# A three-stage transformer kernel: seven masked products in the first mixture, betas by accumulating transfers, one key-value product on VectorE and LayerNorm statistics on ScalarE

## The chip, the cores and the metric

The kernel runs on one core of one Trainium2 chip. A core has five engines that run their own instruction lists and wait for each other by semaphores: TensorE (PE) for matrix products, VectorE (DVE), ScalarE (ACT), GpSimd (POOL) and SyncE (SP), which here only issues transfers. The metric is the device time of one execution in microseconds; the median of 3 runs of the kernel before is 938.53 us (938.17 to 942.1).

## The reference, cut to what matters

The input is 16 sequences of 512 tokens with 128 features. Four blocks follow each other, each with an adaptive LayerNorm ahead of it:

```python
x = L0_attn_x                       # (16, 512, 128)
# block 1: a linear recurrence over the tokens, gated, then LayerNorm with gamma and beta
h = _layernorm(x) * (1 + ca) + sa
x = x + ga * _L0_attn_ref(h, A, Bp, Cp, Dp, Wg, bg, gamma, beta)
# block 2: a mixture of 8 experts, one of them for each token
h = _layernorm(x) * (1 + cb) + sb
sel = argmax(softmax(h @ gate_w + gate_b))
x = x + gb * (h @ expert_w[sel] + expert_b[sel])
# block 3: causal linear attention, 16 heads of 8
h = _layernorm(x) * (1 + ca) + sa
q, k, v = softplus(h @ Wq.T + bq), softplus(h @ Wk.T + bk), h @ Wv.T + bv
kv, k1 = cumsum(k[..., :, None] * v[..., None, :]), cumsum(k)
x = x + ga * ((einsum(q, kv) / sum(q * k1)) @ Wo.T + bo)
# block 4: a mixture of 8 experts with two per token, swiglu, 256 hidden
h = _layernorm(x) * (1 + cb) + sb
```

The scale and shift vectors (`sa`, `ca`, `ga`, `sb`, `cb`, `gb`) are one row of 128 per sequence. `_layernorm` takes mean and variance over the 128 features of a token.

## The kernel before

A sequence is C = 4 tiles of 128 tokens. `x_tok` holds all of x, 128 tokens by 64 tiles by 128 features, in SBUF for the whole kernel. There are five phases, each a block of engine lists with a barrier behind it, and within a phase the lists are written out by hand in the order in which each engine works.

**Phase 1 (0 to about 101 us)** builds the powers of the state matrix and the gated, normalised input. `roots(i)` on GpSimd (L241, L243) takes the square roots of the variances for a group of four sequences, four times. **Phase 2 (to 147 us)** is the recurrence as Toeplitz products, in 16 groups of U = 4 features' matrices. For each group VectorE spreads the ends of chunks over `carry` in three copies (L666), and TensorE multiplies them (L706).

**The first mixture (147 to 345 us)** joins block 1's output to x and does block 2 for one sequence w after the other. VectorE: `statistics` of block 1's output (L1007, L1011), `gamma` (L1035 in the head, L1040 later: normalised times ga*gamma), `joined` (L1050 in the head, L1054 later: add to x_tok), `stats_x` (L1018, L1022), `shift_x_head` (L1027), `best` (L1061 to L1073: add the gate's bias to the logits, find the largest, make a one-hot `hot`), and `mask(w, e)` (L1091): the sequence's features `f_t` times the one-hot row of expert e, which has been spread over all partitions in `wide`. `added` (L1082) adds the experts' output. TensorE: `turn` (L1125, transposes of the normalised tokens), `logits` (L1133), `turn_hot` (L1141), `bias` (L1157, the one-hot times the experts' biases, split into three bf16 pieces), `product(w, e)` (L1161, expert e's weights times masked features, accumulated over e in PSUM) and `turn_back` (L1149). Each product shows as two instructions in the profile. GpSimd has four-column means and scales for the later LayerNorms (L844 to L867) and `beta(w)` (L884), which adds the row ga*beta to x_tok. ScalarE: `squares` with accumulated sums (L925), `norm_y`, `norm_x` (L949, L959), `feat` (L967) and `scaled` (L980). In the head, before the first product, TensorE does idle products (L70) between its steps. SyncE loads the rows ga*gamma and ga*beta of each sequence four ahead (`rows`), all weights at the phase's start, and sends each one-hot to DRAM and back (`kept`, `spread`).

**Attention (345 to 707 us)** is a loop over n = 0 to 20 in which each step works on several sequences at once: the step names below carry the lag. VectorE, in the list's order: `weighted(n-1, 0)` (L1983, queries times running key-value sums in PSUM), `denominators` (L1989), `correction(n)` (L1994, a part of softplus), `weighted(n-1, 1)`, `logits(n-5)` (L2076) with the choice of two experts, `corrected`, `softplus(n)` (L2001, L2007), `residual(n-2)` (L2032: x_tok gets the attention's output), `weighted(n-1, 2)`, `states(n)`, `shifted(n-3)` (L2051), `gated` (L2065), `weighted(n-1, 3)`, `moments(n-2)` (L2038, L2044: mean and variance of the four tiles), then `first_cum` (L2013), `added`, `modulated(n-3)` (L2057, L2059) and `divided(n-1)` (L1974). GpSimd makes four key-value products per sequence, `products(w, c)` (L1641), c = 0 to 3, and sends the tokens' rows by indirect transfers, `send` (L1650). TensorE turns each product into running sums, `sums(w, c)` (L2450), 16 half products. ScalarE, among others: `payload` (L1715, L1717), `turned_pay` (L1834), `norm0` (L1723), `normed` (L1821), `variance_log` and `variance_root` (L1692, L1697: the LayerNorm scale from `moments`) and `squares` of the next norm (L1803).

**The second mixture (707 to 943 us)** runs 71 tiles of tokens sorted by expert.

## Time and profile before

| | us |
|---|---|
| median of 3 runs | 938.53 (938.17 to 942.1) |
| the profiled execution's own time | 945.22 |
| its span, on which all rows stand | 943.4 |

| stretch, us from the span's start | what | length | PE busy | DVE busy | ACT busy | POOL busy |
|---|---|---|---|---|---|---|
| 0 to 147.3 | phases 1 and 2 | 147.3 | 124.7 | 106.0 | 63.0 | 17.9 |
| 147.3 to 178.6 | first mixture, head | 31.3 | 26.8 | 30.0 | 14.0 | 14.9 |
| 178.6 to 337.6 | first mixture, products | 159.0 | 152.5 | 146.5 | 113.2 | 100.6 |
| 337.6 to 345.0 | its end | 7.4 | 5.5 | 0.9 | 2.3 | 1.7 |
| 345.0 to 440.4 | attention, first turns | 95.4 | 90.7 | 75.3 | 62.4 | 40.8 |
| 440.4 to 643.8 | attention, ten full turns | 203.4 | 192.7 | 190.7 | 147.2 | 166.4 |
| 643.8 to 707.0 | attention, last turns | 63.2 | 51.6 | 57.3 | 34.7 | 50.2 |
| 707.0 to 943.4 | second mixture | 236.4 | 213.9 | 167.4 | 181.3 | 174.1 |

An engine's busy time is the time in which it executed. TensorE's matmuls overlap, so the start of the next tells its pace better than a duration does. Where TensorE does idle products, its busy time says nothing about need.

### The profile page before, as it was taken

To read this page: it belongs to the slowest core of one execution; us is meant where nothing else is said; L and a number is where in the kernel's file an instruction comes from. 1 tells how busy PE (TensorE), PEld (TensorE's weight loads), DVE (VectorE), ACT (ScalarE), POOL (GpSimd) and SP (SyncE) were. 2 spreads that over 40 slices of the span, in tenths; PEclk is the share of its full clock that TensorE was granted. 3 is DMA by queue.
4 is the path that set the end of the run, shared out by engine and by line. 5 is a ranking of instruction groups with operands and counts; after the bars stand their busy time and mean duration, and the time that the engine had idled before them with its cause. 6 is when DMAs were issued, how large, how long until landed. Compare 5 with 4: busy or idle time off the path is not lost.

```text
span 943.4 us, 24125 instructions
## 1 busy us (share of the span) xinstructions
PE 858.5 (91%) x7676; PEld 674.7 (72%) x7692; DVE 774.1 (82%) x2369; ACT 618.2 (66%) x1603; POOL 566.4 (60%) x547
## 2 busy tenths in 40 slices
PE   6979898998999989999999999999879999999990
PEld 5945576645445458888778877787668888888890
DVE  3988787999999736988999999999886866666996
ACT  3557123487888446467677777666557888888880
POOL 1211004277776414443888888888777777777773
PEclk9989999899999999999999999999998999999996
DMA  5330262233223203001111112111227766756987
GB/s 155 95 95 1 67 204 59 104 110 141 102 101 130 99 3 96 15 17 35 43 52 49 49 54 64 53 50 49 66 68 219 219 183 183 228 181 196 338 263 248
DMA packets 93962, 105.82 MB, mean 112 GB/s; under 512 B 16095, under 2 KB 75802, under 8 KB 91661
## 3 DMA queue, kind: packets, MB, share of 16 engines
q1 hardware_dynamic: 81884, 84.59, 29.3%
q0 software_dynamic: 8640, 17.97, 5.3%
q10 hardware_dynamic: 3312, 1.70, 0.6%
q8 instruction: 64, 1.05, 0.5%
q14 instruction: 62, 0.50, 0.2%
HBM read 79.91 MB, written 24.32 MB: 110 GB/s over the span
## 4 chain that ended last, share of the span: by engine, by line
PE 48%; DVE 8%; issue 2%; ACT 2%; DMA 2%; POOL 1%; SPq 0%; ACTq 0%; DVEq 0%; POOLq 0%
PE ps L2694 12%; PE ps L2450 10%; PE ps L2717 6%; PE ps L2466 2%; PE ps L2513 2%; PE ps L2441 2%; PE ps L2416 2%; PE ps L2677 2%; PE ps L2567 2%; PE ps L2551 2%; PE ps L2429 1%; DVE qk L2001 1%; DVE qk L2007 1%; PE ps L2461 1%; DMA parts<-gx,dest 1%
## 5 line engine op out<-in xcount | busy, mean ns | idle before, releaser
L1641 POOL TENSOR_TENSOR kvb<-qk,v 128x1024 f32<-128x1024 f32 x64 | 127.3, 1995 | 68.8 <-DVE qk L2007 48.9
L1650 POOL DMA_INDIRECT rows_of<-payb,posu x128 | 144.3, 1128 | 40.1 <-issue 27.5
L2450 PE MATMUL ps<-con,kvb 128*128 128x128 f32 x1024 | 126.0, 276 | 0.0
L1161 PE MATMUL ps<-masked,ew 128*128 128x512 f32 x256 | 123.3, 610 | 1.9 <-DVE masked L1091 1.8
L2450 PEld LDWEIGHTS ps<-con,kvb 128*128 128x128 f32 x1024 | 119.4, 192 | 1.0 <-issue 1.0
L2378 DVE TENSOR_SCALAR qk<-ps,b 128x256 f32<-128x256 f32 x142 | 62.1, 478 | 49.7 <-PE ps L2694 44.6
L1674 POOL DMA_INDIRECT parts<-h,dest x72 | 80.6, 1119 | 23.3 <-issue 20.1
L1674 POOL DMA_INDIRECT parts<-gx,dest x70 | 78.7, 1125 | 21.3 <-issue 19.2
L1091 DVE TENSOR_TENSOR masked<-f_t,wide 128x512 f32<-128x512 f32 x128 | 85.9, 715 | 4.9 <-PE ps L1161 4.7
L1983 DVE TENSOR_TENSOR qc<-ps,qk 128x1024 f32<-128x1024 f32 x64 | 78.0, 1218 | 9.3 <-PE ps L2450 8.2
L1161 PEld LDWEIGHTS ps<-masked,ew 128*128 128x128 f32 x256 | 44.8, 192 | 44.9 <-issue 30.0
L2717 PE MATMUL ps<-w,f_t 128*128 x568 | 75.1, 275 | 0.0
L2717 PEld LDWEIGHTS ps<-w,f_t 128*128 128x128 f32 x568 | 69.0, 192 | 8.2
L1888 ACT ACTIVATE qk<-ps,b 128x256 f32<-128x256 f32 x142 | 59.6, 470 | 18.3 <-PE ps L2694 17.9
L2694 PE MATMUL ps<-qd,ex 128*128 128x256 f32 x288 | 69.8, 386 | 0.0
L2694 PE MATMUL ps<-qd,lg 128*128 128x256 f32 x280 | 66.2, 379 | 0.0
L70 PE MATMUL ps<-con 128*128 128x128 f32 x398 | 56.3, 293 | 5.5 <-PEq L75 3.9
L70 PEld LDWEIGHTS ps<-con 128*128 128x128 f32 x398 | 51.4, 204 | 9.6 <-issue 6.8
L2694 PEld LDWEIGHTS ps<-qd,ex 128*128 128x128 f32 x288 | 53.0, 194 | 6.0
L1893 ACT ACTIVATE nrm<-qk,limit 128x512 f32<-128x512 f32 x71 | 51.3, 722 | 6.8
L2267 DVE SCALAR_TENSOR_TENSOR f_t<-qk,nrm 128x512 f32<-128x512 f32 x71 | 49.2, 693 | 6.8 <-DVE qk L2378 0.5
L2694 PEld LDWEIGHTS ps<-qd,lg 128*128 128x128 f32 x280 | 50.5, 190 | 5.4
(370 smaller groups left out, 2107.0 us busy)
## 6 DMA issues: line engine op xcount, KB each, us to landing
wide<-hot_dram SPq DMA_DIRECT2D x16, 1024.0 KB, 4.6
kvb<-rows_of SPq DMA_DIRECT2D x71, 132.0 KB, 2.5
ex<-in_w_dram SPq DMA_DIRECT2D x36, 256.0 KB
lg<-in_w_dram SPq DMA_DIRECT2D x35, 256.0 KB
toep<-taps_dram SPq DMA_DIRECT2D x16, 512.0 KB, 4.5
xg<-parts SPq DMA_DIRECT2D x16, 512.0 KB, 5.2
x_tok<-in_x_dram SPq DMA_DIRECT2D x16, 256.0 KB, 2.9
rb<-den_dram SPq DMA_DIRECT2D x64, 64.0 KB
```

Of the source, the lines that this page charges most:

```text
L70: nc.tensor.matmul(ps[:, bank, 0:P], k("ident"), k("ident"), start=True, stop=True)
L1091: nc.vector.tensor_tensor(masked[e % 4][:, :], f_t[w % W][:, :], wide[w % W][:, e, :], ALU.mult).then_inc(s["masked"], 1)
L1161: nc.tensor.matmul(ps[:, w % 2, :], ew0[:, e, :], masked[e % 4][:, :], start=False, stop=(e == E - 1)).then_inc(s["product"], 1)
L1641: nc.gpsimd.tensor_tensor(kv[g % KB][:, :, :].rearrange("p e (h d) -> p e h d", h=H), k_in, v_in, ALU.mult).then_inc(s["kv"], 1)
L1650: nc.gpsimd.indirect_dma_start(rows_of, bass.IndirectOffsetOnAxis(ap=posu[w % PR][:, slot, t:t + 1], axis=0), pay[w % PB][:, t, :], None). ...
L1674: nc.gpsimd.indirect_dma_start(parts, bass.IndirectOffsetOnAxis(ap=dest[:, at, c:c + 1], axis=0), yw[u][:, c, :], None).then_inc(s_out[u], 16)
L1888: last = nc.scalar.activation(glu[v % 2][:, f, :], ps[:, bank, f * SP:(f + 1) * SP], ACT.Relu, bias=b1[:, bass.ds(e * NF + f, 1)], scale=-1.0)
L1983: nc.vector.tensor_tensor(qc[g % 2][:, :, :], cum(g), q_in, ALU.mult).then_inc(s["qc"], 1)
L2378: last = nc.vector.tensor_scalar(lin[v % 2][:, f, :], ps[:, bank + 1, f * SP:(f + 1) * SP], b1[:, bass.ds(e * NF + 2 + f, 1)], 8.0, ALU.ad ...
L2450: last = nc.tensor.matmul(cum(g)[:, e, :], kv[g % KB][:, e, :], k("upto"), start=True, stop=True)
L2694: last = nc.tensor.matmul(ps[:, bank + f // 2, (f % 2) * SP:(f % 2 + 1) * SP], w1c[v % WC][:, f * P:(f + 1) * P], x_t[v % 2][:, :], start= ...
L2717: last = nc.tensor.matmul(to, act_t[v % 2][:, j, c * P:(c + 1) * P], w2[:, bass.ds(e * (2 * D) + j * D, D)], start=False, stop=(c == S - 1 ...
```

## The change

In phase 1 and at ten places GpSimd now issues `add_beta(b)`, a transfer that adds the row ga*beta to the four tiles of sequence b in x_tok as it writes (b = 0 to 9): five ahead of the last `roots` and five behind. The other six are `late_beta` transfers in the first mixture; `joined(w)` for w from 10 waits for all six. `beta` on GpSimd is gone, and the row load brings only ga*gamma.

In phase 2 the three carry copies are one. The mixture's weights and biases are loaded and prepared here, and GpSimd subtracts the last expert's weights from the seven others' (128 x 896). The mixture then computes the last expert's product for all tokens, unmasked (`base`), and seven masked products with the differences. The gate's bias enters by a bf16 product ahead of the logits, so `best` reads PSUM. The lists of all five engines are in a new order.

In attention `last_product(n-1)` on VectorE makes the fourth key-value product. `moments` is gone; ScalarE makes sums, negative means and centred squares of the tokens instead.

```diff
+                    def add_beta(b):
+                        pool.wait_ge(s_nt, b + 1)
+                        nc.gpsimd.dma_start(x_tok[:, b * C:(b + 1) * C, :], bass.AP(rows_tensor, (b * len(ROWS) + 1) * D, [[0, P], [0, C], [1, D]]),
+                                            accum_op=ALU.add).then_inc(betas_added, 16)
+                    for i in range(NI - 1):
                         roots(i)
+                    pool.wait_ge(s_rout, 16)
+                    for b in range(U + 1):
+                        add_beta(b)
+                    roots(NI - 1)
+                    for b in range(U + 1, EARLY_BETAS):
+                        add_beta(b)
...
-                                for c in range(1, C):
-                                    src = by_chunk(ends[u][:, :], c - 1)
-                                    last = nc.vector.tensor_tensor(
+                                src = ends[u][:, :].rearrange("p (b c) -> p b c", c=C)[:, :, 0:C - 1]
+                                nc.vector.tensor_tensor(
...
+                    pool.wait_ge(s_ahead, 6 * 16)
+                    nc.gpsimd.tensor_tensor(ew0[:, 0:M, :], ew0[:, 0:M, :], ew0[:, M:E, :].to_broadcast([P, M, D]), ALU.subtract).then_inc(s_ew, 1)
...
-                    def beta(w):
-                        if exists(w):
-                            landed(pool, s_rows, w)
-                            nc.gpsimd.tensor_tensor(tiles(x_tok, w), tiles(x_tok, w), rows[w % W][:, 1:2, :].to_broadcast([P, C, D]), ALU.add).then_inc(s["beta"], 1)
+                    def late_beta(w):
+                        nc.gpsimd.dma_start(tiles(x_tok, w), bass.AP(rows_tensor, (w * len(ROWS) + 1) * D, [[0, P], [0, C], [1, D]]),
+                                            accum_op=ALU.add).then_inc(s["late_betas"], 16)
...
+                            if w >= EARLY_BETAS:
+                                dve.wait_ge(s["late_betas"], (B - EARLY_BETAS) * 16)
                             done(dve, "gamma", w)
-                            done(dve, "beta", w)
...
-                            nc.vector.tensor_tensor(logit[:, :, :], ps[:, LOGIT, 0:C * E].rearrange("p (t e) -> p t e", e=E),
-                                                    gb0[:, :, :].to_broadcast([P, C, E]), ALU.add).then_inc(s["lg"], 1)
...
+                    def base(w):
+                        done(pe, "moe_t", w - 2)
+                        done(pe, "feat", w)
+                        nc.tensor.matmul(ps[:, w % 2, :], ew0[:, M, :], f_t[w % W][:, :], start=True, stop=False).then_inc(s["plain"], 1)
...
+                    def row_sums(w):
...
+                            for c in range(C):
+                                last = nc.scalar.activation(unread[:, c, :], tile(w, c), ACT.Copy, accum_out=sx[:, c:c + 1])
+                    def centred_squares(w):
...
+                            for c in range(C):
+                                last = nc.scalar.activation(unread[:, c, :], tile(w, c), ACT.Square, bias=nm[w % 2][:, c:c + 1], accum_out=vs[w % 2][:, c:c + 1])
...
                         payload(n - 7)
+                        row_sums(n - 5)
+                        negative_means(n - 5)
+                        centred_squares(n - 5)
                         turned_pay(n - 7)
...
+                    def last_product(w):
...
+                            nc.vector.tensor_tensor(kv[g % KB][:, :, :].rearrange("p e (h d) -> p e h d", h=H), k_in, v_in, ALU.mult).then_inc(s["kv_last"], 1)
...
                         denominators(n - 1)
+                        last_product(n - 1)
                         correction(n)
...
                         weighted(n - 1, 3)
-                        moments(n - 2)
```

The order at three places. First VectorE at the start of the first mixture, before:

```order
L1007 BN_STATS halves<-xg 128x6 x4
L1011 BN_AGGR moments<-halves 128x2 x4
L1007 BN_STATS halves<-xg 128x6 x4
L1011 BN_AGGR moments<-halves 128x2 x4
L1035 SCALAR_TENSOR_TENSOR yn_88<-xg,moments,rows_73 128x128 x4
L1050 SCALAR_TENSOR_TENSOR x_tok<-yn_88,stat_77,x_tok 128x128 x4
L1018 BN_STATS halves_x<-x_tok 128x6 x4
L1022 BN_AGGR moments_x<-halves_x 128x2 x4
L1035 SCALAR_TENSOR_TENSOR yn_89<-xg,moments,rows_74 128x128 x4
L1027 SCALAR_TENSOR_TENSOR stat_82<-moments_x,stat_81 128x4
L1050 SCALAR_TENSOR_TENSOR x_tok<-yn_89,stat_77,x_tok 128x128 x4
```

The same place now (`statistics`, `gamma`, `joined`, `stats_x` are L1036 and L1040, L1064, L1080, L1047 and L1051):

```order
L1036 BN_STATS halves<-xg 128x6 x4
L1040 BN_AGGR moments<-halves 128x2 x4
L1064 SCALAR_TENSOR_TENSOR yn_93<-xg,moments,rows_79 128x128 x4
L1080 SCALAR_TENSOR_TENSOR x_tok<-yn_93,stat_83,x_tok 128x128 x4
L1047 BN_STATS halves_x<-x_tok 128x6 x4
L1051 BN_AGGR moments_x<-halves_x 128x2 x4
L1036 BN_STATS halves<-xg 128x6 x4
L1040 BN_AGGR moments<-halves 128x2 x4
L1056 SCALAR_TENSOR_TENSOR stat_88<-moments_x,stat_87 128x4
L1064 SCALAR_TENSOR_TENSOR yn_94<-xg,moments,rows_80 128x128 x4
L1080 SCALAR_TENSOR_TENSOR x_tok<-yn_94,stat_83,x_tok 128x128 x4
```

The second sequence's statistics moved from ahead of the first gamma to behind the first sequence's stats_x.

Second, TensorE where one sequence's products end and the next one's begin, before:

```order
L1161 MATMUL ps<-masked_106,ew_65 128x512
L1161 MATMUL ps<-masked_107,ew_65 128x512
L1125 MATMUL ps<-con,xn_90 128x128 x4
L1161 MATMUL ps<-masked_108,ew_65 128x512
L1161 MATMUL ps<-masked_109,ew_65 128x512
L1133 MATMUL ps<-gw_71,f_t_92 128x8 x4
L1157 MATMUL ps<-hot_b_98,ebx 128x512
L1149 MATMUL ps<-con,moe_t_105 128x128 x4
L1161 MATMUL ps<-masked_106,ew_65 128x512
L1161 MATMUL ps<-masked_107,ew_65 128x512
```

The same now (L1191 the masked products, L1183 `base`, L1158 the gate's bias, L1187 the experts' bias):

```order
L1191 MATMUL ps<-masked_114,ew_5 128x512
L1152 MATMUL ps<-con,xn_95 128x128 x4
L1191 MATMUL ps<-masked_111,ew_5 128x512
L1191 MATMUL ps<-masked_112,ew_5 128x512
L1183 MATMUL ps<-f_t_99,ew_5 128x512
L1158 MATMUL ps<-gb_13,one_14 128x32
L1161 MATMUL ps<-gw_18,f_t_97 128x8 x4
L1187 MATMUL ps<-hot_b_103,ebx 128x512
L1177 MATMUL ps<-con,moe_t_110 128x128 x4
L1191 MATMUL ps<-masked_113,ew_5 128x512
```

The next sequence's accumulation, which began with the bias product L1157, now begins with the unmasked product L1183.

Third, attention. VectorE from the fourth weighting of one sequence to the second of the next, before (L1989 the denominators, L1994 the correction):

```order
L2038 BN_STATS st<-x_tok 128x6 x4
L2044 BN_AGGR mv_174<-st 128x2 x4
L2013 TENSOR_TENSOR qd<-ps,qk_189 128x512
L2070 TENSOR_TENSOR x_tok<-x_tok,gx_210 128x512
L2027 TENSOR_TENSOR skv_199<-skv_199 128x144 x2
L2057 TENSOR_TENSOR h_208<-h_208,rows_168 128x512
L2059 TENSOR_TENSOR h_208<-h_208,rows_168 128x512
L1974 TENSOR_TENSOR g_t<-ps,rb_202 128x512
L1983 TENSOR_TENSOR qc_195<-ps,qk_189 128x1024
L1989 RECIPROCAL rden_201<-ps 96x128
L1994 SCALAR_TENSOR_TENSOR ex<-lg,ex 128x1024
L1983 TENSOR_TENSOR qc_196<-ps,qk_189 128x1024
```

The same now (L2045 is `last_product`, L2051 the denominators, L2056 the correction):

```order
L2075 TENSOR_TENSOR qd<-ps,qk_191 128x512
L2119 TENSOR_TENSOR x_tok<-x_tok,gx_214 128x512
L2089 TENSOR_TENSOR skv_201<-skv_201 128x144 x2
L2106 TENSOR_TENSOR h_212<-h_212,rows_171 128x512
L2108 TENSOR_TENSOR h_212<-h_212,rows_171 128x512
L2025 TENSOR_TENSOR g_t<-ps,rb_206 128x512
L2034 TENSOR_TENSOR qc_198<-ps,qk_191 128x1024
L2051 RECIPROCAL rden_203<-ps 96x128
L2045 TENSOR_TENSOR kvb<-qk_191,v_195 128x1024
L2056 SCALAR_TENSOR_TENSOR ex<-lg,ex 128x1024
L2034 TENSOR_TENSOR qc_199<-ps,qk_191 128x1024
```

The statistics and aggregates went, and one 128 x 1024 product stands between the denominators and the correction.

ScalarE in the same turn, from the payload on, before:

```order
L1715 ACTIVATE payb<-h_209,rm_183 128x128 x4
L1717 ACTIVATE payb<-place 128x4
L1834 ACTIVATE p_t<-ps 128x512
L1723 ACTIVATE nrm_184<-x_tok,shift_61,rs_60 128x128 x4
L1730 ACTIVATE ex<-ps,bq 128x512
L1821 ACTIVATE h_208<-x_tok,sh_180,rv_177 128x128 x4
```

And now (L1714, L1722 and L1729 are the sums, negative means and centred squares, L1882 the turned payload):

```order
L1761 ACTIVATE payb<-h_212,rm_186 128x128 x4
L1763 ACTIVATE payb<-place 128x4
L1714 ACTIVATE unread,sx<-x_tok 128x128 x4
L1722 ACTIVATE nm_174<-sx 128x4
L1729 ACTIVATE unread,vs_176<-x_tok,nm_174 128x128 x4
L1882 ACTIVATE p_t<-ps 128x512
L1769 ACTIVATE nrm_187<-x_tok,shift_75,rs_74 128x128 x4
L1776 ACTIVATE ex<-ps,bq 128x512
L1869 ACTIVATE h_211<-x_tok,sh_183,rv_180 128x128 x4
```

The three new rows stand between the payload and its turn.

## Rows read from the trace of the kernel before

**Rows 1.** Busy time by stretch: length, then busy us and instructions of each engine.

```profile
147.30:178.60 31.30, 26.83 (x176) 23.78 (x176) 29.95 (x122) 14.03 (x36) 14.86 (x21) 0.84 0.32 101
178.60:337.60 159.00, 152.54 (x543) 75.75 (x543) 146.53 (x527) 113.20 (x357) 100.64 (x164) 0.99 0.28 106
```

**Rows 2.** In time: start, us, engine; and a line's group: busy us, mean ns.

```profile
75.86 0.26 POOL L241 TENSOR_SCALAR rstd<-mv 128x16 f32<-128x16 f32 x1 [20.03 <-DVE mv L261]
...
L1650 POOL DMA_INDIRECT rows_of<-payb,posu x128 | 144.3, 1128 | 40.1 <-issue 27.5
```

**Rows 3.** In time, the mixture's head: VectorE and GpSimd.

```profile
150.31 2.55 POOL L884 TENSOR_TENSOR x_tok<-x_tok,rows 128x512 f32<-128x512 f32 x2 [2.60 <-DMA rows<-rows_dram]
150.97 2.74 DVE L1035 SCALAR_TENSOR_TENSOR yn<-xg,moments,rows 128x128 f32<-128x128 f32 x4
...
159.42 4.93 POOL L884 TENSOR_TENSOR x_tok<-x_tok,rows 128x512 f32<-128x512 f32 x4
...
162.00 2.37 DVE L1027 SCALAR_TENSOR_TENSOR stat<-moments_x,stat 128x4 f32<-128x4 f32 x1
164.29 1.44 DVE L1035 SCALAR_TENSOR_TENSOR yn<-xg,moments,rows 128x128 f32<-128x128 f32 x4
...
177.88 4.30 DVE L1091 TENSOR_TENSOR masked<-f_t,wide 128x512 f32<-128x512 f32 x7
```

**Rows 4.** In time, TensorE in the mixture.

```profile
248.93 0.60 PE L1125 MATMUL ps<-con,xn 128*128 128x128 f32 x4
249.36 1.88 PE L1161 MATMUL ps<-masked,ew 128*128 128x512 f32 x4
251.08 0.99 PE L1133 MATMUL ps<-gw,f_t 128*128 128x8 f32 x8
252.00 0.38 PE L1157 MATMUL ps<-hot_b,ebx 24*128 24x512 bf16 x1
```

**Rows 5.** In time, VectorE in the mixture.

```profile
243.55 0.18 DVE L1061 TENSOR_TENSOR logit<-ps,gb 128x32 f32<-128x32 f32 x1
...
257.82 4.76 DVE L1091 TENSOR_TENSOR masked<-f_t,wide 128x512 f32<-128x512 f32 x6
```

**Rows 6.** In time, one turn of attention.

```profile
524.99 0.19 DVE L2076 TENSOR_TENSOR logit<-ps,gb 128x32 f32<-128x32 f32 x1 [0.30 <-PE ps L2616]
...
530.00 0.68 DVE L2032 TENSOR_TENSOR x_tok<-x_tok,ps 128x512 f32<-128x512 f32 x1
530.23 0.97 PE L2567 MATMUL ps<-v,qk 128*128 128x144 f32 x6 [0.90 <-DVE qk L2007]
533.59 0.60 ACT L1834 ACTIVATE p_t<-ps 128x512 f32<-128x512 f32 x1 [3.99 <-PE ps L2538]
534.86 0.86 DVE L2038 BATCH_NORM_STATS2 st<-x_tok 128x6 f32<-128x128 f32 x4
538.15 1.95 PE L2450 MATMUL ps<-con,kvb 128*128 128x128 f32 x16
539.72 1.98 POOL L1641 TENSOR_TENSOR kvb<-qk,v 128x1024 f32<-128x1024 f32 x1
540.13 1.22 DVE L1983 TENSOR_TENSOR qc<-ps,qk 128x1024 f32<-128x1024 f32 x1
543.80 1.22 DVE L1983 TENSOR_TENSOR qc<-ps,qk 128x1024 f32<-128x1024 f32 x1 [0.50 <-PE ps L2450]
545.32 0.19 DVE L2076 TENSOR_TENSOR logit<-ps,gb 128x32 f32<-128x32 f32 x1 [0.30 <-PE ps L2616]
```

**Rows 7.** ScalarE's accumulating passes, grouped by line: busy us, mean ns, idle before.

```profile
L925 ACT ACTIVATE junk<-x_tok,stat 128x128 f32<-128x128 f32 x112 | 43.3, 388 | 13.4 <-DVE x_tok L1082 11.5 <-DVE x_tok L1054 1.8
L925 ACT ACTIVATION_READ_ACCUMULATOR junk<-x_tok,stat 128x1 f32 x112 | 21.0, 187 | 0.0
L1803 ACT ACTIVATE junk<-h 128x128 f32<-128x128 f32 x64 | 18.8, 298 | 3.7 <-DVE h L2059 3.7
```

**Rows 8.** In time, ScalarE in attention's last turns.

```profile
682.80 0.60 ACT L1834 ACTIVATE p_t<-ps 128x512 f32<-128x512 f32 x1 [0.86 <-PE ps L2538]
```

384 lines of the change are left out of this document (201 added, 183 removed).

## The prediction

> **What bounds the kernel now.** I read four views in this order. The busy times by stretch say which engine fills a stage. The instructions in order of time say who waits for whom there. The groups by line give the price of one instruction. The groups' idle columns bound what a wait is worth.
>
> The first mixture has two parts. In its head, from the barrier at 147.3 to the first product at 178.6, VectorE is busy 29.95 of 31.30 us and nothing else fills the time [rows 1]: the head ends when VectorE has worked through its list. From 178.6 to 337.6 TensorE (152.54) and VectorE (146.53 of 159.00) are both nearly full [rows 1]. To see which one sets the pace, take starts and not modelled busy times: four half products go by in 251.08 - 249.36 = 1.72 us, 0.43 each; four transposes take 0.43, the logits 0.92, and the bias product at most its 0.38 [rows 4]. I take 0.31 for that one, where the next start falls. A sequence is 16 halves (6.88), three sets of transposes (1.3), logits and bias: 9.4 us. Less what is done in the head, that is about 144 us of TensorE work in 159; the 15 us over are waits on VectorE. VectorE's list is about 149 us, of which 5.6 are stalls: six masks from 257.82 took 4.76 where seven from 177.88 took 4.30, so 0.61 each and 3.67 for six [rows 3, 5]; 1.09 us went while GpSimd added a beta. Five such places and a small one make 5.6.
>
> In attention the same turn repeats from 524.99 to 545.32, 20.33 us [rows 6]; eleven such turns are in the steady part. The ring: the state product on TensorE waits 0.90 us for a VectorE product at 530.23; from there TensorE runs on to the sums that end at 540.10, the first weighting on VectorE starts at 540.13, the second at 543.80 after 0.50 us of waiting, the logits at 545.32 after 0.30 [rows 6]; from there VectorE's list runs without a gap to the product that releases the next state product. Whatever sits on VectorE between 540.1 and 545.3 beyond those small waits lengthens every turn.
>
> **Phase 1: nothing.** Five accumulating transfers go on GpSimd ahead of its last square root, which starts at 75.86 after 20.03 us of idling [rows 2]. Their cost there is not in the trace. The nearest row is the indirect transfer, 128 descriptors in 1.128 us [rows 2]; these have 512 short rows each, so at most 4 x 1.128 = 4.5 us, 5 x 4.5 = 22.6. The fifth sequence is ready about 15 us before 75.86 and the shift that reads the root comes near 80: the queue is done in time, or within 3 us of it. Below: 0, above: +3. I take 0, since 4 x is already a price for four whole transfers.
>
> **Phase 2: nothing.** Three carry copies become one, which shortens VectorE's part of each group; but TensorE sets the pace of the scan, and VectorE waits for it in every group. That same slack covers what the weight differences, the bias pieces and the six loads on GpSimd and SyncE might hold up. If the cover went, a held VectorE would show as carry waits on TensorE; I keep +-0.5 us for it.
>
> **Mixture, head: -3.1.** Three rows show what beta on GpSimd costs VectorE. The first gamma took 2.74 us, a later one of the same shape 1.44 (1.3 lost); a shift of four columns took 2.37 us while GpSimd ran four betas from 159.42 (2.2 lost) [rows 3]; smaller ones make 3.9. Also gone are two logit additions (0.4), one shift that goes behind the first masks (0.25), and the wait for a constant at the start (0.4): -5.0. Against it, one statistics is no longer ahead of the first gamma, so gamma waits for its row, which lands at 150.3 [rows 3], about 1.0; and the shorter list meets the roots of ScalarE sooner, about 0.9. The first product moves from 178.6 to 175.5.
>
> The Trainium skill ("SBUF — State Buffer", the section on the port pair that VectorE and GpSimd share) says that a GpSimd operation and a VectorE operation with two SBUF inputs exclude each other for a whole instruction; rows 3 agree (2.37 us for a tiny one). By that rule the gain of taking betas off GpSimd is real, and it speaks against the product that attention puts on VectorE.
>
> **Mixture, products: -11.5.** VectorE loses 16 masks (16 x 0.61 = 9.8), 14 further logit additions at 0.2 (2.9) [rows 3, 5] and the 5.6 of stalls: 149 becomes about 131. TensorE keeps all halves: the unmasked product with the last expert's weights is one of the eight. Two of the plain products move into the head (2 x 0.86 = -1.7), the gate bias adds 14 small products, about +1. TensorE needs about 143.5, VectorE 131: TensorE becomes the bound, and only waits for single masks or hot rows stay, for which I leave 4 us. 159.0 becomes 147.5. Six late transfers sit in GpSimd's queue among means and scales; each up to 4.5 us [rows 2]. If they cost that, roots and with them normalised rows come late for two or three sequences. Bounds of the term: -14 (2 us of waits) and -4 (most waits replaced). I choose near the upper third, because the plain products give TensorE work exactly when masks are not there yet.
> Mixture: -3.1 - 11.5 = -14.6.
>
> **Attention: +6.6.** The fourth key-value product moves from GpSimd, where one takes 1.98 us [rows 6], to VectorE. There it is of the weighting's shape (128 x 1024, at most 1.22 us); I take 1.15. It stands behind the denominators and ahead of the correction, so in the stretch above: 1.15 - 0.50 delays the second weighting by 0.65, and the logits by 0.35 after their 0.30. The moments, 0.86 for the statistics at 534.86 and a third of one for the aggregates, leave VectorE, but just ahead of 540.13, where it waits for TensorE's 540.10 anyway [rows 6]: they buy nothing there. Part of the 0.35 is taken up behind, since the VectorE list from 545 to 530 is no longer held by GpSimd's fourth product. I count 0.25.
>
> ScalarE gets sums, means and centred squares. Four accumulating passes without bias at 0.298 and four with bias at 0.388, their read-outs overlapped [rows 7], and a small one of 0.2: by durations 4 x 0.298 + 0.2 + 4 x 0.388 = 2.9, with the two hand-overs about 3.2 us. They can start when the residual is written, 530.00 + 0.68 = 530.7, and stand ahead of the payload's turn, which before ran at 533.59 after 3.99 us of idling [rows 6]: 2.9 us of room. The 0.3 over goes on to the normalised tokens and is nearly eaten before 540.1: 0.05. Together 0.3 a turn, 11 turns: +3.3. The first turns, in which engines are less full, +0.6. In the last turns there is no filling work: at 682.80 the turned payload starts after only 0.86 us of idling [rows 8], so the block's 3.2 us delays it by some 2.7 once, and routing's last logits behind it. +3.3 + 0.6 + 2.7 = +6.6, between +3 (tail +0.5, turns +0.2) and +10 (0.6 a turn).
>
> GpSimd's third product ends at 541.70 and the new one on VectorE can't start before weighting and reciprocal, near 542.2 [rows 6]. A turn in which GpSimd is 0.5 us later makes VectorE wait.
>
> **Sum.** 0 + 0 - 14.6 + 6.6 = -8.0. The profiled run's own time is 945.2 (span 943.4 and 1.8 around it); it becomes 937.2. The median of the runs shown is 938.5, 6.7 under it; the same difference gives 930.5. The second mixture is untouched.
>
> **Rivals.** (a) The mixture gives only the head and little more: the late transfers cost near 4.5 us each and TensorE waits at other places instead. -3.1 - 4.5 = -7.6, total 938.5 - 7.6 + 6.6 = 937.5. For it: GpSimd's chain for a sequence is already four steps long. Against it: VectorE gets 18 us of room. 0.22.
> (b) The new product costs attention nothing but the tail (0.1 a turn, +3.3 in all), and the mixture fills TensorE (-17): 938.5 - 17 + 3.3 = 924.8. 0.20.
> (c) Slower: the statistics on ScalarE are longer than their room. If each of the eight read-outs adds to its pass instead of lying beneath it, the block is 4 x 0.487 + 0.2 + 4 x 0.575 = 4.5 us by bounds from [rows 7], 1.6 over the room; the normalised tokens, their modulation and the division follow, and the first weighting starts 1.3 later each turn: 11 x (1.3 + 0.25) + 3.3 = +20, total 938.5 - 14.6 + 20 = 943.9; with (a)'s mixture 951. It decides from a block of about 4.0 us. Against it: 64 passes without and 112 with a bias now run back to back with no idle time ahead of a read-out [rows 7]. 0.09.
> (d) The transfers don't do what they say on time: an accumulating transfer takes over 4.7 us on GpSimd, and the last root and its shift come late, +3 to +8: 933.5 to 938.5. 0.05.
>
> **How the numbers follow.** The forecast, 930.5 with its own range of 926.5 to 934, has 0.44. 0.5% of the median, about what a measurement of this kernel can tell from no change, is 4.7: the bounds are 933.8 and 943.2. Forecast and (b) are faster, and a small part of (a) and (d): 0.44 + 0.20 + 0.03 = 0.67. The rest of (a) and (d), and (c) at its mildest, within half a percent: 0.24 + 0.01 = 0.25. Slower: what is left of (c), 0.08. The range reaches from (b) to behind (a): 923 to 941.
>
> **What would show it.** Right: the first product near 175.5 and products over 147 to 149 us; the VectorE operations of the head back at 1.44 and 0.13; TensorE's waits on masks gone; the turn of attention at 20.5 to 20.8; ScalarE's block at 3.0 to 3.4 us. Wrong: a turn of 21 or more (c), or product waits on normalised rows behind a GpSimd transfer (a). Most open is how long GpSimd holds an accumulating transfer; no row shows one.

## The result, and the profile after

The changed kernel takes 947.03 us (median of 20 runs, 941.49 to 950.57); the kernel before, run beside it, 941.31 (20 runs). The ratio is 1.0044, 95% interval 1.0025 to 1.0062: 4.1 us slower by the ratio (the two medians differ by 5.7), where I had forecast 8.0 us faster and a range from 923 to 941. The profiled execution has a span of 945.7 us.

The profile before, on which the prediction rests, was itself a long execution (span 943.4). The kernel before was profiled once more; that span was 937.1, and the difference lies where the argument does not rest: phase 1 took 98.4 us instead of 101.5, phase 2 44.8 instead of 46.2, the second mixture 231.7 instead of 233.1. So stages are compared with both, and a stage read from one profile can be off by 1 to 3 us there. A stage ends where its marker begins: phase 2 with GpSimd's clearing of `carry`, the head with the first statistics, products with the first mask and so on to the last masked product, attention's start with its first `norm0`, then corrections 0, 5 and 15, and the first product of the second mixture.

| stage, us | before | before, again | after | after to again | forecast |
|---|---|---|---|---|---|
| phase 1 | 101.5 | 98.4 | 98.8 | +0.4 | 0 |
| phase 2 | 46.2 | 44.8 | 45.2 | +0.4 | 0 |
| mixture, head (to the first mask) | 30.1 | 30.1 | 27.0 | -3.1 | -3.1 |
| mixture, products | 159.9 | 159.9 | 162.1 | +2.2 | -11.5 |
| its end, and attention's start to correction 0 | 15.8 | 15.8 | 17.9 | +2.1 | 0 |
| attention, corrections 0 to 5 | 86.8 | 86.8 | 90.2 | +3.4 | } |
| attention, corrections 5 to 15 | 203.4 | 203.4 | 204.6 | +1.3 | } +6.6 |
| attention, last turns | 66.5 | 66.2 | 67.6 | +1.5 | } |
| second mixture | 233.1 | 231.7 | 232.2 | +0.5 | 0 |

The head came out as forecast in sum. VectorE there, after (start, us; in brackets the idle time before and what ended it):

```profile
147.29 1.44 DVE L1064 SCALAR_TENSOR_TENSOR yn<-xg,moments,rows 128x128 f32<-128x128 f32 x4 [1.61 <-DMA rows<-rows_dram]
...
158.14 0.13 DVE L1056 SCALAR_TENSOR_TENSOR stat<-moments_x,stat 128x4 f32<-128x4 f32 x1
```

The gamma that took 2.74 us is at 1.44, the four-column shift that took 2.37 at 0.13 [rows 3]. The first gamma waits 1.61 us for its row, which the prediction had foreseen at about 1.0.

The products did not. TensorE in that stretch, after: two places with a wait, and what follows them.

```profile
203.44 0.63 PE L1152 MATMUL ps<-con,xn 128*128 128x128 f32 x4 [2.00 <-ACT xn L987]
...
204.62 3.43 PE L1191 MATMUL ps<-masked,ew 128*128 128x512 f32 x4
...
231.14 6.47 PE L1191 MATMUL ps<-masked,ew 128*128 128x512 f32 x10 [6.03 <-DVE masked L1121]
...
244.63 4.46 PE L1191 MATMUL ps<-masked,ew 128*128 128x512 f32 x10
```

Four half products take 3.43 us behind the first wait, where four took 1.88 before [rows 4]. Ten take 6.47 behind the second and 4.46 later on. The granted clock says why (columns: stretch, length, busy us and instructions of PE, PEld, DVE, ACT, POOL; then PEclk, DMA share, GB/s):

```profile
201.00:206.00 5.00, 3.00 (x12) 1.72 (x11) 2.91 (x14) 4.35 (x15) 1.61 (x5) 0.83 0.44 57
206.00:212.00 6.00, 6.00 (x22) 2.75 (x21) 3.29 (x20) 4.14 (x17) 5.60 (x10) 0.86 0.73 199
212.00:225.00 13.00, 13.00 (x63) 7.32 (x60) 11.51 (x50) 12.38 (x40) 11.71 (x21) 1.00 0.48 61
225.00:231.00 6.00, 0.11 (x2) 0.00 (x0) 0.61 (x1) 2.55 (x6) 2.49 (x5) 0.77 0.92 207
231.00:238.00 7.00, 6.86 (x15) 3.30 (x16) 5.75 (x17) 3.67 (x12) 2.61 (x4) 0.71 0.72 183
```

After its first wait TensorE works on at a mean 0.83 and 0.86 of full speed. Then it idles six microseconds and works on at 0.71: each time it ran partly at the lower level of 1.2 GHz. The two waits cost 8.0 us and the slower work behind them about 1.6 and 2.0. VectorE had not been late with the masks. It waited too, for a transfer:

```profile
211.87 2.50 DVE L1121 TENSOR_TENSOR masked<-f_t,wide 128x512 f32<-128x512 f32 x4 [1.52 <-DMA wide<-hot_dram]
...
230.39 2.50 DVE L1121 TENSOR_TENSOR masked<-f_t,wide 128x512 f32<-128x512 f32 x4 [6.39 <-DMA wide<-hot_dram]
```

`wide` is the one-hot row spread over all partitions; SyncE first stores the 8 KB of one-hot rows (`kept`), waits for them to land, then issues the spread. SyncE's queue, before and then after:

```profile
209.32 0.28 SPq L818 DMA_DIRECT2D hot_dram<-hot_b  x1
210.68 0.32 SPq L823 DMA_DIRECT2D wide<-hot_dram  x1
```

```profile
199.68 0.29 SPq L869 DMA_DIRECT2D hot_dram<-hot_b  x1
206.59 0.32 SPq L874 DMA_DIRECT2D wide<-hot_dram  x1
...
213.73 0.29 SPq L869 DMA_DIRECT2D hot_dram<-hot_b  x1
219.61 0.32 SPq L874 DMA_DIRECT2D wide<-hot_dram  x1
...
220.68 3.03 SPq L869 DMA_DIRECT2D hot_dram<-hot_b  x1
231.57 0.32 SPq L874 DMA_DIRECT2D wide<-hot_dram  x1
```

From store to spread it was 1.36 us, and 1.34 for the next pair. Now it is 6.9, 5.9 and 10.9 (there the issue of the store alone took 3.03), and 4.6 for the pair behind it. What SyncE waited for a store to land, from 195 to 240 us (us in total, times, longest), before and then after:

```profile
SPq L789 <- DMA hot_dram<-hot_b: 4.0, 4, 1.0
SPq L823 <- DMA hot_dram<-hot_b: 1.0, 1, 1.0
```

```profile
SPq L840 <- DMA hot_dram<-hot_b: 24.1, 4, 7.8
```

So four stores take 24.1 us to land, up to 7.8 for one, where five took 5.0. What is new on the transfer queues at that time is `late_beta`: GpSimd issued them at 193.37, 197.72, 207.10, 210.53, 216.88 and 222.55. The last of its rows, and the summary of transfers from 190 to 232 us, after:

```profile
222.55 1.35 POOL L933 DMA_DIRECT2D x_tok<-rows_dram  x1
```

```profile
wide<-hot_dram SPq DMA_DIRECT2D x4, 1024.0 KB, 5.1
x_tok<-rows_dram POOLq DMA_DIRECT2D x6, 256.0 KB, 9.6
```

Each holds GpSimd for some 1.35 us and lands 9.6 us (median) after it was issued, almost twice the 5.1 us of a spread of four times the bytes.

### The profile page after: what moved, and what is told of

Read it like the earlier page. It is cut to its first block and busy times, and to the rows that moved or that the text cites. A ratio compares the mean times of both kernels' runs of the same rounds, so it can differ in the third digit from the quotient of the medians.

```text
span 945.7 us, 24089 instructions
## 1 busy us (share of the span) xinstructions
PE 853.9 (90%) x7630; PEld 671.6 (71%) x7646; DVE 761.7 (81%) x2193; ACT 665.0 (70%) x1875; POOL 546.0 (58%) x541
## 3 DMA queue, kind: packets, MB, share of 16 engines
q8 instruction: 63, 1.03, 0.5%
## 5 line engine op out<-in xcount | busy, mean ns | idle before, releaser
L1673 POOL DMA_INDIRECT rows_of<-payb,posu x128 | 165.7, 1295 | 41.2 <-issue 29.2
L1664 POOL TENSOR_TENSOR kvb<-qk,v 128x1024 f32<-128x1024 f32 x48 | 95.0, 1989 | 83.2 <-DVE qk L2069 82.7
L1191 PE MATMUL ps<-masked,ew 128*128 128x512 f32 x224 | 106.6, 613 | 6.7 <-DVE masked L1121 6.6
L1696 POOL DMA_INDIRECT parts<-h,dest x72 | 73.8, 1025 | 30.6 <-issue 18.4
L1696 POOL DMA_INDIRECT parts<-gx,dest x70 | 74.0, 1057 | 28.2 <-issue 18.9
L1121 DVE TENSOR_TENSOR masked<-f_t,wide 128x512 f32<-128x512 f32 x112 | 73.1, 686 | 16.8 <-PE ps L1191 8.2
L1191 PEld LDWEIGHTS ps<-masked,ew 128*128 128x128 f32 x224 | 41.0, 196 | 46.1 <-issue 33.5
L2746 PE MATMUL ps<-qd,lg 128*128 128x256 f32 x280 | 66.2, 379 | 0.0
L73 PE MATMUL ps<-con 128*128 128x128 f32 x336 | 54.2, 320 | 8.3 <-PEq L78 5.7
## 6 DMA issues: line engine op xcount, KB each, us to landing
x_tok<-rows_dram POOLq DMA_DIRECT2D x16, 256.0 KB, 10.2
```

The source lines that it names most:

```text
L73: nc.tensor.matmul(ps[:, bank, 0:P], k("ident"), k("ident"), start=True, stop=True)
L1121: nc.vector.tensor_tensor(masked[at % 4][:, :], f_t[w % W][:, :], wide[w % W][:, e, :], ALU.mult).then_inc(s["masked"], 1)
L1191: nc.tensor.matmul(ps[:, w % 2, :], ew0[:, e, :], masked[(w * M + e) % 4][:, :], start=False, stop=(e == M - 1)).then_inc(s["product"], 1)
L1664: nc.gpsimd.tensor_tensor(kv[g % KB][:, :, :].rearrange("p e (h d) -> p e h d", h=H), k_in, v_in, ALU.mult).then_inc(s["kv"], 1)
L1673: nc.gpsimd.indirect_dma_start(rows_of, bass.IndirectOffsetOnAxis(ap=posu[w % PR][:, slot, t:t + 1], axis=0), pay[w % PB][:, t, :], None). ...
L1696: nc.gpsimd.indirect_dma_start(parts, bass.IndirectOffsetOnAxis(ap=dest[:, at, c:c + 1], axis=0), yw[u][:, c, :], None).then_inc(s_out[u], 16)
```

## The experiments

All ratios are with the kernel before, run beside them on the same chip; stages are read from one profile of each kernel with the markers above. A ratio and the quotient of two medians differ by up to 0.3 per cent here.

| kernel | median us | ratio, 95% | phase 1 | phase 2 | head | products | corr. 0-5 | 5-15 | last turns |
|---|---|---|---|---|---|---|---|---|---|
| old_attention | 940.8 | 1.0009 (0.9988-1.0031) | 98.1 | 45.9 | 26.8 | 162.4 | 87.9 | 203.5 | 65.2 |
| attention_only | 947.4 | 1.0066 (1.0037-1.0096) | 98.8 | 44.8 | 30.1 | 158.4 | 89.3 | 204.6 | 66.7 |
| betas16 | 944.6 | 1.0048 (1.0024-1.0071) | 111.5 | 45.5 | 26.8 | 150.4 | 90.5 | 204.6 | 66.2 |
| betas16_old_attention | 939.6 | 0.9989 (0.9966-1.0012) | 110.2 | 46.7 | 26.7 | 152.1 | 87.8 | 203.5 | 65.2 |
| late_gpsimd | 932.0 | 0.9873 (0.9829-0.9917) | 100.7 | 46.0 | 26.8 | 152.7 | 88.0 | 203.5 | 65.2 |
| all_gpsimd | 935.6 | 0.9918 (0.9885-0.9950) | 98.2 | 44.6 | 30.9 | 156.3 | 87.9 | 203.4 | 65.5 |
| late_plain | 941.3 (1 run) | | 97.9 | 45.1 | 27.1 | 160.0 | 89.4 | 204.6 | 66.2 |
| product_only | 942.1 | 1.0006 (0.9978-1.0034) | 97.4 | 44.9 | 30.1 | 158.5 | 89.1 | 204.7 | 64.6 |
| statistics_only | 944.0 | 1.0018 (0.9985-1.0051) | 98.4 | 44.9 | 30.1 | 158.4 | 87.7 | 203.1 | 68.0 |
| betas_phase2 | 940.7 | 0.9989 (0.9956-1.0023) | 97.8 | 58.3 | 26.8 | 150.4 | 87.9 | 203.4 | 66.0 |
| late_gpsimd_idle18 | 931.5 (1 run) | | 100.8 | 46.0 | 26.9 | 152.7 | 86.8 | 203.5 | 65.8 |
| before_again | 938.9 (1 run) | | 98.4 | 44.8 | 30.1 | 159.9 | 86.8 | 203.4 | 66.2 |

### The two halves of the change

`old_attention` is the changed kernel with every edit of attention taken back; `attention_only` is the kernel before with these edits alone. What the one has and the other lacks:

```diff
-                        products(n, 3)
+                        row_sums(n - 5)
+                        negative_means(n - 5)
+                        centred_squares(n - 5)
+                        last_product(n - 1)
-                        moments(n - 2)
```

> The new phases 1 and 2 and the new first mixture, with attention as before. In the changed kernel the trace put the start of attention 4.2 us earlier than before, and the start of the second mixture 3.2 us later, so 7.4 us were lost between. Theory: the attention part of the change alone costs 5 to 6 us (3.4 in the first five turns, 1.2 in the next ten, about 1 behind), and the rest of the 7.4 is the 1.6 us by which the mixture's end hands over. Then this kernel is 5 to 6 us faster than the changed one and 1 to 3 us faster than before. Rival: what attention loses is inherited from the mixture (clock, late transfers), and the attention part is free; then this kernel is as slow as the changed one.

> The kernel before with the attention part of the change alone. By the theory above 5 to 6 us slower than before: the first five turns 90.2 instead of 86.8 us, ten turns 204.6 instead of 203.4. By the rival no slower than 1 us.

`old_attention` is 6.2 us faster than the changed kernel by the medians. The rival of the first run falls: attention's part costs by itself, 0.66% (6.2 us, between 3.5 and 9.0) where the theory said 5 to 6; its first five turns took 89.3 us where 90.2 were expected. The rest of the change (phases 1 and 2 and the mixture) gives nothing: ratio 1.0009, where I had expected 1 to 3 us. So the 14.6 us that the prediction put there are what is missing.

### Where the mixture's gain went

`betas16` has sixteen early transfers and no late one:

```diff
-        EARLY_BETAS = 10
+        EARLY_BETAS = 16
...
-                    ... late_beta(10); ... late_beta(11); ... late_beta(12); ... late_beta(13); ... late_beta(14); ... late_beta(15); ...
```

> The changed kernel with all sixteen betas added by transfers in phase 1 and none in the mixture. Theory: the six late transfers, 256 KB each in 512-byte pieces, fill the transfer queues, the 8 KB one-hot rows queue behind them (6 to 11 us instead of 1.3 from their issue to the spread's), and VectorE's masks wait 7.9 us, TensorE 6.0 and then runs at a lower clock. Then products take 150 us (first mask to last product) instead of 162, no mask waits for a transfer, and the kernel is 10 to 12 us faster than the changed one. Rival 1: it is the 1.3 us that each transfer holds GpSimd, which delays the means and scales: the wait of 2.0 us for normalised rows goes, the 6.0 too, but 3 to 5 us at most come back. Rival 2: the new order itself makes the one-hot late; then the wait stays at its place and less than 2 us come back. Against the gain: six more transfers run beside phase 2's loads; if they hold those, phase 2 gets up to 4 us longer.

The first theory holds for the products: 150.4 instead of 162.1 us, with no mask that waits for a transfer; SyncE waits 5.4 us for five stores (208 to 253 us), and TensorE's wait for normalised rows is 0.20 us. VectorE's waits from 183 to 245 us are short, and for TensorE:

```profile
222.88 0.29 DVE L1108 SCALAR_TENSOR_TENSOR x_tok<-x_tok,ps 128x128 f32<-128x128 f32 x1 [0.51 <-PE ps L1175]
224.60 0.69 DVE L1119 TENSOR_TENSOR masked<-f_t,wide 128x512 f32<-128x512 f32 x1 [0.17 <-PE ps L1189]
232.08 0.19 DVE L1090 TENSOR_REDUCE largest<-ps 128x4 f32<-128x32 f32 x1 [0.50 <-PE ps L1159]
```

But the kernel is 0.5% slower than before and by the medians only 2.4 us faster than the changed one, not 10 to 12. The price moved to the end of phase 1, which is 12.7 us longer; I had allowed up to 4, and in phase 2, which stayed at 45.5. GpSimd and TensorE there:

```profile
76.15 11.78 POOL L267 DMA_DIRECT2D x_tok<-rows_dram  x9
88.73 1.28 POOL L267 DMA_DIRECT2D x_tok<-rows_dram  x1 [0.80 <-PE ps L532]
101.58 1.30 POOL L267 DMA_DIRECT2D x_tok<-rows_dram  x1 [11.57 <-issue]
111.52 1.92 POOL L715 MEMSET carry<- 128x512 f32 x4 [8.65 <-POOLq L212]
```

```profile
111.56 1.97 PE L754 MATMUL ps<-xg,states_of 128*64 128x256 f32 x8 [13.44 <-PEq L212]
```

Nine transfers issue back to back at 1.3 us each; the last has 11.57 us of idling in front of it that no other engine ended. By then the earlier ones had drained: from 101.0 to 102.9 us the profile shows not one transfer packet. The last lands 9.0 us after its issue, at 110.6, and the barrier opens at 111.5. That GpSimd stood because its queue was full is my reading; no run varied the number.

`betas16_old_attention` has attention as before too, and 18 idle products at the mixture's end.

> The same with attention as before and 18 idle products instead of 14 at the mixture's end. If the two parts add up: 10 to 12 and 5 to 6 us, and 1.6 of hand-over, together 16 to 19 us faster than the changed kernel, 11 to 14 faster than before. If the mixture's gain were lost again in attention (the rival of the first run), no faster than the changed kernel by more than 8 us.

Products 152.1, and with phase 1 at 110.2 the gain is gone in the same way: 0.9989, and 7.5 us faster than the changed kernel by the medians. The parts do not add up to the 16 to 19 us expected, because phase 1 takes 12 of them.

`betas_phase2` also has attention as before and 18 idle products. It issues the last six transfers on GpSimd in phase 2, behind the bias pieces, where GpSimd has nothing else to do:

```diff
+                    for b in range(EARLY_BETAS, B):
+                        nc.gpsimd.dma_start(x_tok[:, b * C:(b + 1) * C, :], bass.AP(rows_tensor, (b * len(ROWS) + 1) * D, [[0, P], [0, C], [1, D]]),
+                                            accum_op=ALU.add).then_inc(betas_added, 16)
+                    pool.wait_ge(betas_added, B * 16)
```

> Attention as before, 18 idle products at the mixture's end, the last six betas by accumulating transfers issued on GpSimd in phase 2, behind the bias pieces. Theory: the transfers hurt only what stands in their queue; in phase 2 GpSimd idles over 50 us. Products 150 to 151 us, head 26.8, phase 2 longer by less than 2: 926 to 931 us, faster than with six additions on GpSimd. Rival: they hold the Toeplitz loads of phase 2 as they held the one-hot rows (6 to 11 us): phase 2 longer by 5 or more, no gain.

The rival was right. Products take 150.4, phase 2 takes 58.3 instead of 45.9: TensorE waits for the Toeplitz loads. TensorE's waits for them (us in total, times, longest), then the transfers from 100 to 155 us:

```profile
PE ps L775 <- DMA toep<-taps_dram: 9.9, 2, 7.7
```

```profile
toep<-taps_dram SPq DMA_DIRECT2D x12, 512.0 KB, 7.3
x_tok<-rows_dram POOLq DMA_DIRECT2D x6, 256.0 KB, 15.9
```

Without the six transfers the twelve loads land in 3.9 us (`old_attention`, 100 to 147 us, otherwise the same phase 2):

```profile
toep<-taps_dram SPq DMA_DIRECT2D x12, 512.0 KB, 3.9
```

Three places for the six transfers, and each time the stage pays: 12 us in phase 1, where the barrier opens only after the last has landed, 12 in phase 2, where loads come late, and 10 to 12 in the mixture, where stores do.

`late_plain` asks whether it is the addition. The late transfers write the same bytes to a tile of their own, so the kernel leaves out the last six betas:

```diff
-                        nc.gpsimd.dma_start(tiles(x_tok, w), bass.AP(...), accum_op=ALU.add).then_inc(s["late_betas"], 16)
+                        nc.gpsimd.dma_start(aside[w - EARLY_BETAS][:, :, :], bass.AP(...)).then_inc(s["late_betas"], 16)
```

> The changed kernel, but the six late transfers write the same bytes in the same pieces to a tile of their own, without adding (the last six sequences' betas are left out of the result). If it is the addition that makes them slow, they land in 3 to 5 us instead of 9.6, the one-hot rows wait 2 us at most and products take 152. If it is the pieces (2048 elements of 512 bytes on GpSimd's queue), nothing changes: landing 9 us, products 160 to 162.

It is hardly the addition (one run): they land in 8.5 us instead of 9.6, SyncE waits 24.5 us for four stores from 195 to 240 us, and products take 160.0.

```profile
aside<-rows_dram POOLq DMA_DIRECT2D x6, 256.0 KB, 8.5
```

```profile
SPq L841 <- DMA hot_dram<-hot_b: 24.5, 4, 10.0
```

But the pieces did not stay the same, as the expectation had it (a transfer has 128 x 4 = 512 pieces of 512 bytes, not 2048). GpSimd's queue from 190 to 232 us (packets, MB, share of 16 engines), in the changed kernel and then in `late_plain`:

```profile
q0 software_dynamic: 3052, 1.52, 33.4%
```

```profile
q0 software_dynamic: 480, 1.57, 53.6%
```

Without the addition the same bytes went in a sixth of the packets, and they took a larger share of the queues. So the run took away the addition and the small pieces together, and the stores stayed late. What it is in a transfer issued by GpSimd that makes it drain for some 9 us stays open.

`late_gpsimd` keeps the ten early transfers and lets GpSimd add the last six betas itself, from a row load of both rows as before:

```diff
-                        nc.gpsimd.dma_start(tiles(x_tok, w), bass.AP(rows_tensor, ...), accum_op=ALU.add).then_inc(s["late_betas"], 16)
+                        landed(pool, s_rows, w)
+                        nc.gpsimd.tensor_tensor(tiles(x_tok, w), tiles(x_tok, w), rows[w % W][:, 1:2, :].to_broadcast([P, C, D]), ALU.add).then_inc(s["late_betas"], 1)
...
-                            if w >= EARLY_BETAS:
-                                dve.wait_ge(s["late_betas"], (B - EARLY_BETAS) * 16)
+                            if w >= FIRST_LATE:
+                                dve.wait_ge(s["late_betas"], w - FIRST_LATE + 1)
```

> Attention as before; phases 1 and 2 and the mixture as in the change, but the six late betas are additions by GpSimd again (behind the row load, as before the change), not transfers. Theory: the late transfers cost the mixture its gain. Without them, and with no extra transfers in phase 1, the products' stage (first mask to last product) takes 150 to 153 us instead of 162.4, the start of phase 2 stays where it is, and the kernel is 9 to 12 us faster than the one with the late transfers, 1.0 to 1.3 percent faster than before. Rival: the new order without slack for GpSimd's additions (1.3 to 1.7 us each, VectorE held for about 1.1) gives half of it away: 155 to 158.

Products 152.7, inside the 150 to 153 expected, head 26.8: 932.0 us, 1.3% faster than before (0.8 to 1.7%), which is 12 us by the ratio and 9.5 by the medians. It beats both kernels. `old_attention` differs from it only in how and when these six additions are made, with the waits and the row load that go with them. It is 8.8 us slower by the medians, and its products alone take 9.7 us more: that is what six late transfers cost.

`all_gpsimd` does all sixteen betas this way, with no accumulating transfer:

```diff
-                    for b in range(U + 1):
-                        add_beta(b)
...
-                    for b in range(U + 1, EARLY_BETAS):
-                        add_beta(b)
...
-                    moments_mean(4); moments_scale(4); mean_2(0); ...
+                    late_beta(0); ...; late_beta(7); moments_mean(4); moments_scale(4); mean_2(0); ...; late_beta(8); mean_2(1); ...
```

> The same with no accumulating transfer at all: all sixteen betas are GpSimd additions in the mixture. This is the seven masked products and the new order alone. Head 30 to 31 us instead of 26.8 (the held gammas and shifts come back), products 151 to 154; in all 3 to 4 us slower than with ten early transfers, still 5 to 8 us faster than before. If the head also stays at 27 the early transfers bought nothing.

As expected in size: 0.8% faster than before, 3.6 us slower than `late_gpsimd`; head 30.9, but products 156.3 where 151 to 154 were expected. The early ten transfers are worth 4.1 us in the head and 3.6 in the products. The seven masked products and the new order alone are worth the other 2 to 4 us of products.

`late_gpsimd_idle18` differs from `late_gpsimd` in one number at the mixture's end:

```diff
-                    idle_products(FREE, 14)
+                    idle_products(FREE, 18)
```

> The fastest kernel so far (six late betas as GpSimd additions, attention as before) with 18 idle products instead of 14 at the mixture's end. In its profile TensorE fell to the lower clock at the barrier (10.2 us from attention's start to the first correction instead of 8.55). If four more idle products hold the clock, it is 8.55 and the kernel 1.6 us faster; two kernels with 14 kept the clock, so it may be chance.

8.55 us from attention's start to the first correction, and 86.8 us for the next stage instead of 88.0; but one run of 931.5 against a median of 932.0 shows no gain of 1.6 us. The two profiles of the same attention, 14 and then 18 idle products:

```profile
343.69:431.65 87.96, 86.37 (x892) 75.40 (x893) 70.83 (x113) 56.01 (x106) 40.30 (x20) 0.96 0.15 37
```

```profile
342.19:428.99 86.80, 84.53 (x887) 74.25 (x893) 71.99 (x113) 56.02 (x106) 40.27 (x20) 0.98 0.15 38
```

The granted clock differs, 0.96 and 0.98, and with it TensorE's busy time, 86.37 and 84.53 us. That four idle products do it isn't shown: `betas16` and `all_gpsimd` have 14 and took 8.55 too, and `betas16_old_attention` has 18 and took 87.8. What decides the clock there stays open; it moves 1 to 1.6 us at a time.

`before_again` is the kernel before, unchanged.

> The kernel before, profiled once more. In the profile that the prediction rests on phase 1 took 2.7 us longer than in every later run and the first five turns of attention 86.8 us where three kernels with the same attention take 87.9. If these are accidents of one execution, this profile has phase 2 at 98 to 99 us, products of 158.4 and 87.9 us for the five turns. If 86.8 comes back, the changed mixture hands something over to attention that costs 1.1 us.

86.8 came back, and products 159.9, against the expectation of 87.9 and 158.4; phase 1 did come to 98.4. By that expectation the changed mixture hands 1.1 us to attention, but `late_gpsimd_idle18` has the new mixture and 86.8 too. Three kernels with the same mixture code but other attention code have 158.4 or 158.5. From 178 to 218 us the granted clock was 0.96 in both profiles of the kernel before and 1.00 in `attention_only`'s; the 1.5 us go with the clock.

### What attention costs

`product_only` is the kernel before with the fourth key-value product on VectorE:

```diff
-                        products(n, 3)
...
                         denominators(n - 1)
+                        last_product(n - 1)
                         correction(n)
```

> The kernel before with only the last key-value product moved to VectorE; moments stay on VectorE. The whole attention part costs 2.5 us in the first five turns, 0.12 a turn in the next ten and 1 to 2 behind. If it is the product that costs the turns, this kernel has 204.6 or more for ten turns (VectorE now carries 1.15 more a turn and nothing leaves it: up to 21.5 us a turn, 215 for ten). If the statistics cost them, ten turns stay at 203.4.

`statistics_only` is the kernel before with the statistics on ScalarE:

```diff
                         payload(n - 7)
+                        row_sums(n - 5)
+                        negative_means(n - 5)
+                        centred_squares(n - 5)
...
-                        moments(n - 2)
```

> The kernel before with the LayerNorm statistics on ScalarE alone; GpSimd makes all four products. With the product alone ten turns took 204.7 us and the tail 64.6, with both 204.6 and 66.7. Theory: the turns are the product's, the tail the statistics': ten turns 203.4 here, tail about 67, first five turns 88.0 to 88.5. Rival: the statistics cost the turns too, hidden under the product: then ten turns are over 204.

With the product ten turns take 204.7, with both 204.6, with the statistics 203.1. The last turns take 64.6, 66.7 and 68.0, against 66.2 before. So the turns are the product's and the tail is the statistics', as the theory had it; but the product shortened the tail by 1.6 us, where 1 to 2 more had been expected. The first five turns are shared: 89.1 and 87.7 against 86.8. All this stands on one profile each: by their ratios (1.0006 and 1.0018, intervals in the table) neither half alone is told from no change.

The part of the product in a turn can be read. VectorE in one turn of `product_only`:

```profile
514.53 1.23 DVE L1984 TENSOR_TENSOR qc<-ps,qk 128x1024 f32<-128x1024 f32 x1
515.67 0.94 DVE L2001 RECIPROCAL rden<-ps 96x128 f32<-96x128 f32 x1
516.54 1.16 DVE L1995 TENSOR_TENSOR kvb<-qk,v 128x1024 f32<-128x1024 f32 x1
517.61 1.21 DVE L2006 SCALAR_TENSOR_TENSOR ex<-lg,ex 128x1024 f32<-128x1024 f32 x1
518.74 1.21 DVE L1984 TENSOR_TENSOR qc<-ps,qk 128x1024 f32<-128x1024 f32 x1
```

No wait is left: the 1.16 us of the product fill the 0.50 and 0.30 of before [rows 6], and TensorE's wait for the state product's input is 1.03 instead of 0.90. The turn is 0.13 us longer.

And `moments` bought next to nothing when they left (203.1 against 203.4 for ten turns), but not only for the reason that I had given. VectorE and GpSimd in `product_only`, where `moments` (L2050) are still there:

```profile
509.26 0.86 DVE L2050 BATCH_NORM_STATS2 st<-x_tok 128x6 f32<-128x128 f32 x4
...
511.02 0.93 DVE L2082 TENSOR_TENSOR x_tok<-x_tok,gx 128x512 f32<-128x512 f32 x1
```

```profile
509.42 1.98 POOL L1641 TENSOR_TENSOR kvb<-qk,v 128x1024 f32<-128x1024 f32 x1
```

and in `statistics_only`, where they are gone:

```profile
509.16 0.68 DVE L2042 TENSOR_TENSOR qd<-ps,qk 128x512 f32<-128x512 f32 x1
509.76 2.12 DVE L2086 TENSOR_TENSOR x_tok<-x_tok,gx 128x512 f32<-128x512 f32 x1
```

```profile
509.33 1.98 POOL L1643 TENSOR_TENSOR kvb<-qk,v 128x1024 f32<-128x1024 f32 x1
```

The addition to x_tok has two inputs in SBUF; moved 1.2 us ahead it meets GpSimd's second product and is done only when that is over, 2.12 us instead of 0.93. The 1.2 us taken from VectorE came back to within a tenth as a hold. The changed kernel shows the same 2.10 at 535.82. It is the exclusion that the prediction took from the Trainium skill ("SBUF — State Buffer", "Who interferes with whom"); these rows agree with it once more: GpSimd's product ends at 511.31, the addition at 511.88.

## Why the prediction was wrong, point by point

**Phases 1 and 2** (0 and 0): +0.4 each. An accumulating transfer holds GpSimd for 1.3 us, under the bound of 4.5, and ten of them delay nothing that shows in phase 1 (98.8 us, where the two profiles before have 98.4 and 101.5).

**Head** (-3.1): -3.1. The gammas and shifts came back as worked out. `all_gpsimd`, without early transfers, has 30.9 in the head, so without the early transfers the head gains nothing.

**Products** (-11.5, between -14 and -4): +2.2. This is the step that failed: "Six late transfers sit in GpSimd's queue among means and scales; each up to 4.5 us. If they cost that, roots and with them normalised rows come late". I priced a transfer only by the engine that issues it (1.35 us, not 4.5) and put its cost on the queues at nothing, without a reason. That cost was the whole loss: each transfer drains for some 10 us, and meanwhile SyncE waited up to 7.8 us, instead of 1.0, for a store of 8 KB that stood in no row of mine, with VectorE's masks and then TensorE behind it. TensorE's waits of 8.0 us and 3.6 us of slower work behind them account for the 11.7 us that `betas16` gained in this stage. A part of what was named did happen: the wait of 2.0 us for normalised rows follows two `late_beta` issues in GpSimd's list, and it is 0.20 in `betas16`; whether GpSimd's time or the queues made it was not separated. With the transfers out of the way, products take 150.4, 8.0 to 9.5 less than before. So the rest of the term, TensorE as the bound with VectorE relieved, was sound but some 2 to 3 us too large. Rival (a) named these transfers, but by GpSimd's time, and ended at 937.5.

**The hand-over** (no term): +2.1. In the changed kernel TensorE had fallen to the lower clock between the mixture's end and attention's first products: 0.83 of full speed from attention's start to correction 0, against 1.00 in `before_again`, and 10.2 us instead of 8.55. It comes and goes between kernels whose code is the same there: 10.2 in `late_gpsimd`, 8.55 in `all_gpsimd`. What decides it stays open.

**Attention** (+6.6): 3.4 + 1.3 + 1.5 = 6.2 by stages against `before_again`, 6.2 by `attention_only`'s ratio. `old_attention` has the same mixture and is the closer comparison: 2.3 + 1.1 + 2.4 = 5.8. The sum was right and its split was not, so that it came out is in part luck. A turn costs 0.11 to 0.13, not 0.3: of the 0.36 that the product adds over the two waits it fills, two thirds are absorbed ahead of the state product. The first five turns cost 2.3 to 3.4, not 0.6; I did not trace what they wait for. The tail costs 1.5 to 2.4, where 2.7 was forecast. ScalarE's block took 531.07 to 534.17, 3.1 us against 3.2 forecast, so rival (c) had nothing to stand on.

**Second mixture** (0): +0.5.

**The base.** The forecast was a difference put on a median of 938.5. Over 20 runs beside the changed kernel the median before was 941.3, so 2.8 of the distance between 930.5 and 947.0 are the small sample of before. The range would have missed all the same.

## What to carry to other kernels

A transfer is not free because its issuing engine is idle: look up what else is on the transfer queues while it drains, above all small stores that an engine waits for. Here six transfers cost 10 to 12 us in each of the three stages where they were tried, and moving them only chose the stage; six additions on GpSimd itself cost the products 0.6 to 2.3 (152.7 against 152.1 and 150.4 without any beta in the mixture). When work is taken off an engine, see what the next instruction will then run beside: in a list full of two-input VectorE operations beside GpSimd products, 1.2 us taken away came back as a hold of 1.2.
